# Cross-attention on one core: each norm's sum of squares folded over two partition halves, so that one constant matmul serves it

## What is computed

```python
text_p = x @ W_text + b_text;  audio_p = ctx @ W_audio + b_audio
Q = layer_norm(text_p, g1, beta1);  K = layer_norm(audio_p, g2, beta2);  V = audio_p
alpha = softmax(Q @ K.T / sqrt(512))
H = (alpha @ V) @ W_out + b_out
out = layer_norm(H + x, g_out, beta_out)
# layer_norm: (x - mean) * rsqrt(mean((x - mean)**2) + 1e-5) * gamma + beta
```

## Time and profile before

| | |
|---|---|
| time, median of 3 runs | 1315.46 us (1315.35 to 1315.54) |
| the profiled execution | 1315.32 us, its span 1313.5 us |
| PE busy | 1293.2 us (98%) |
| ACT busy | 1014.2 us (77%) |
| DVE busy | 934.8 us (71%) |
| POOL busy | 728.7 us (55%) |

### The profile page before, as it was taken

How to read it: one execution, slowest core, us unless ns; L and a number is a source line. 1 busy time by engine, 2 the same in 40 slices (tenths; PEclk the granted TensorE clock), 3 DMA queues, 4 the chain that set the end, 5 groups by cost and what they waited for, 6 DMA issues and landing times.

```text
span 1313.5 us, 22669 instructions
## 1 busy us (share of the span) xinstructions
PE 1293.2 (98%) x6960; PEld 1104.6 (84%) x6960; DVE 934.8 (71%) x1537; ACT 1014.2 (77%) x1655; POOL 728.7 (55%) x757
## 2 busy tenths in 40 slices
PE   7999999999999999999999999999999999999996
PEld 5688888888888888888888888888888888888885
DVE  6577666777667777667776667776667776667777
ACT  6678777788777887787887777887777887778873
POOL 1124666555675556675556665556665556755566
PEclk9999999999999999999999999999999999999999
DMA  7454755565755666745657655657655667555682
GB/s 248 121 123 126 200 179 135 155 186 184 200 174 119 170 180 196 199 139 148 169 176 200 192 145 138 188 176 200 185 122 164 184 184 200 166 134 163 180 205 81
DMA packets 76694, 221.04 MB, mean 168 GB/s; under 512 B 9856, under 2 KB 9856, under 8 KB 68480
## 3 DMA queue, kind: packets, MB, share of 16 engines
q1 hardware_dynamic: 55312, 154.70, 33.4%
q0 software_dynamic: 21360, 66.06, 26.4%
HBM read 121.12 MB, written 33.55 MB: 118 GB/s over the span
## 4 chain that ended last, share of the span: by engine, by line
PE 95%; DVE 2%; POOL 1%; DMA 1%; SPq 1%; ACT 1%; issue 0%; DVEq 0%; ACTq 0%
PE wide L295 9%; PE wide L294 9%; PE wide L293 9%; PE score L262 7%; PE score L260 7%; PE score L261 7%; PE wide L262 7%; PE wide L260 7%; PE wide L261 7%; PE wide L342 6%; PE wide L343 6%; PE wide L344 6%; PE score L267 2%; PE turn L262 1%; PE turn L261 1%; PE turn L260 1%
## 5 line engine op out<-in xcount | busy, mean ns | idle before, releaser
L954 POOL TENSOR_TENSOR y_rows<-y_rows,go_row 128x512 f32<-128x512 f32 x120 | 156.9, 1308 | 271.5 <-ACT y_rows L513 271.5
L293 PE MATMUL wide<-xT_hi,wt_hi 128*128 128x512 f32 x512 | 206.8, 404 | 0.7 <-ACT k_cols L482 0.7
L295 PE MATMUL wide<-xT_hi,wt_lo 128*128 128x512 f32 x512 | 202.0, 395 | 0.0
L294 PE MATMUL wide<-xT_lo,wt_hi 128*128 128x512 f32 x512 | 201.8, 394 | 0.0
L481 ACT ACTIVATE squares<-wide,bac_col 128x512 f32<-128x512 f32 x128 | 88.3, 690 | 116.9 <-PE wide L262 116.9
L956 POOL TENSOR_TENSOR y_rows<-y_rows,betao_row 128x512 f32<-128x512 f32 x120 | 165.6, 1380 | 9.4
L694 DVE SCALAR_TENSOR_TENSOR k_cols<-k_cols,g_col,turn 128x512 f32<-128x512 f32 x128 | 92.2, 742 | 100.7 <-ACT turn L499 100.7
L260 PE MATMUL wide<-cT_hi,wa_hi 128*128 128x512 f32 x384 | 152.4, 397 | 0.0
L342 PE MATMUL wide<-wao_hi,pcT_hi 128*128 128x512 f32 x384 | 151.8, 395 | 0.6 <-DVE pcT_lo L648 0.6
L262 PE MATMUL wide<-cT_hi,wa_lo 128*128 128x512 f32 x384 | 152.3, 397 | 0.0
L261 PE MATMUL wide<-cT_lo,wa_hi 128*128 128x512 f32 x384 | 152.1, 396 | 0.0
(11 more groups left out here) (121 smaller groups left out, 3575.2 us busy)
## 6 DMA issues: line engine op xcount, KB each, us to landing
xT_in<-in_xT SPq DMA_DIRECT2D x32, 1024.0 KB, 9.8
y_rows<-in_x_rows SPq DMA_DIRECT2D x124, 256.0 KB, 4.4
xT_lo<-xT_in POOLq DMA_DIRECT2D x31, 1024.0 KB, 7.0
y_rows<-bao_row POOLq DMA_DIRECT2D x31, 1024.0 KB, 10.9
out<-y_rows SPq DMA_DIRECT2D x124, 256.0 KB, 2.3
cT_in<-in_cT SPq DMA_DIRECT2D x32, 768.0 KB, 8.0
c_kept<-in_c_rows SPq DMA_DIRECT2D x32, 768.0 KB, 7.0
q_cols<-in_L_xattn_W_text SPq DMA_DIRECT2D x1, 1024.0 KB, 5.6
```

What stands on the lines that cost most here:

```text
L293: nc.tensor.matmul(wide[h][:], wt_hi[:, d, cols], xT_hi[:, d, :], start=(d == 0), stop=False)
L294: nc.tensor.matmul(wide[h][:], wt_hi[:, d, cols], xT_lo[:, d, :], start=False, stop=False)
L295: done = nc.tensor.matmul(wide[h][:], wt_lo[:, d, cols], xT_hi[:, d, :], start=False, stop=(d == DT - 1))
L954: nc.gpsimd.tensor_tensor(rows, rows, go_row[:], ALU.mult).then_inc(y_scaled, 1)
```

## The change

The 128x512 sum is folded to 64x512 before it is split. ACT copies its upper 64 partitions into the bank that the mean will later be written to (`move_half`), DVE adds them to the lower 64 (`sq_half`), and the split puts the high part in partitions 0 to 63 and the low part in partitions 64 to 127 of one tile `sq_parts`. One matmul with `mean_of` then sums both. The keys' mean matmul stands behind the whole of the query projection h=1 instead of behind its first quarter. Two waits of ACT are for the folded sum instead of the split one.

```diff
             def mean_squares(i, to, parts_made, var):
-                pe.wait_ge(sq_hi_made, i + 1)
-                nc.tensor.matmul(to, mean_of[:], sq_hi[:], start=True, stop=False)
-                pe.wait_ge(sq_lo_made, i + 1)
-                nc.tensor.matmul(to, mean_of[:], sq_lo[:], start=False, stop=True).then_inc(var, 1)
+                pe.wait_ge(parts_made, i + 1)
+                nc.tensor.matmul(to, mean_of[:], sq_parts[:], start=True, stop=True).then_inc(var, 1)
...
-                project_q(i, 1, 0)
-                mean_squares(i, turn[0][:], k_sq_hi, k_sq_lo, k_var)
-                project_q(i, 1, 2)
+                project_q(i, 1)
+                mean_squares(i, turn[0][:], k_sq_parts, k_var)
...
-                wait(act, q_sq_lo if h == 3 else q_summed, i)
+                wait(act, q_halved if h == 3 else q_summed, i)
...
-                act.wait_ge(k_sq_lo if h == 3 else k_summed, i + 1)
+                act.wait_ge(k_halved if h == 3 else k_summed, i + 1)
...
+            def move_half(i, to, summed, moved):
+                act.wait_ge(summed, i + 1)
+                nc.scalar.copy(to[P // 2:P, :], squares[P // 2:P, 3, :]).then_inc(moved, 1)
...
                 k_centre(i, 3)
+                move_half(i, turn[0], k_summed, k_moved)
                 if late:
                     y_norm(i - 2, odd, 0)
...
                 q_centre(i, 3)
+                move_half(i, turn[1], q_summed, q_moved)
                 k_high(i, 3)
...
-            def split_sum(i, var_before, before, summed, hi_made, lo_made):
+            def split_sum(i, of, moved, var_before, before, halved, hi_made, parts_made):
+                half = P // 2
+                dve.wait_ge(moved, i + 1)
+                nc.vector.tensor_tensor(sq_half[:], squares[0:half, 3, :], of[half:P, :], ALU.add).then_inc(halved, 1)
                 wait(dve, var_before, before)
-                dve.wait_ge(summed, i + 1)
-                nc.vector.tensor_copy(sq_hi[:], squares[:, 3, :]).then_inc(hi_made, 1)
+                dve.wait_ge(halved, i + 1)
+                nc.vector.tensor_copy(sq_parts[0:half, :], sq_half[:]).then_inc(hi_made, 1)
                 dve.wait_ge(hi_made, i + 1)
-                low(sq_lo[:], squares[:, 3, :], sq_hi[:]).then_inc(lo_made, 1)
+                low(sq_parts[half:P, :], sq_half[:], sq_parts[0:half, :]).then_inc(parts_made, 1)
```

More of the change, by code:

```diff
@@ L70, in cross_attention_kernel @@
         squares = sb("squares", [P, HT, T * P])
-        sq_hi, sq_lo = sb("sq_hi", [P, T * P], F32R), sb("sq_lo", [P, T * P], F32R)
+        sq_parts, sq_half = sb("sq_parts", [P, T * P], F32R), sb("sq_half", [P // 2, T * P])
         kT_hi, kT_lo = sb("kT_hi", [P, HT, T * P], F32R), sb("kT_lo", [P, HT, T * P], F32R)
@@ L122, in cross_attention_kernel @@
         mean_of_made = sem("mean_of_made")
+        k_moved, q_moved = sem("k_moved"), sem("q_moved")
         k_log, q_log, k_rstd, q_rstd = sem("k_log"), sem("q_log"), sem("k_rstd"), sem("q_rstd")
@@ L130, in cross_attention_kernel @@
         xT_split, cT_split, pT_split, pc_split = sem("xT_split"), sem("cT_split"), sem("pT_split"), sem("pc_split")
-        k_added, k_summed, k_sq_hi, k_sq_lo = sem("k_added"), sem("k_summed"), sem("k_sq_hi"), sem("k_sq_lo")
-        q_added, q_summed, q_sq_hi, q_sq_lo = sem("q_added"), sem("q_summed"), sem("q_sq_hi"), sem("q_sq_lo")
+        k_added, k_summed, k_halved = sem("k_added"), sem("k_summed"), sem("k_halved")
+        q_added, q_summed, q_halved = sem("q_added"), sem("q_summed"), sem("q_halved")
+        k_sq_hi, k_sq_parts, q_sq_hi, q_sq_parts = sem("k_sq_hi"), sem("k_sq_parts"), sem("q_sq_hi"), sem("q_sq_parts")
         k_normed, q_normed = sem("k_normed"), sem("q_normed")
@@ L297, in project_q, with mean_squares @@
                     done.then_inc(q_done, 1)
-            def mean_squares(i, to, sq_hi_made, sq_lo_made, var):
-                pe.wait_ge(sq_hi_made, i + 1)
-                nc.tensor.matmul(to, mean_of[:], sq_hi[:], start=True, stop=False)
-                pe.wait_ge(sq_lo_made, i + 1)
-                nc.tensor.matmul(to, mean_of[:], sq_lo[:], start=False, stop=True).then_inc(var, 1)
+            def mean_squares(i, to, parts_made, var):
+                pe.wait_ge(parts_made, i + 1)
+                nc.tensor.matmul(to, mean_of[:], sq_parts[:], start=True, stop=True).then_inc(var, 1)
             def turn_p(j, b):
@@ L403, in step @@
                     probs_context(j, 2)
-                mean_squares(i, turn[1][:], q_sq_hi, q_sq_lo, q_var)
+                mean_squares(i, turn[1][:], q_sq_parts, q_var)
                 if not first:
@@ L817, in step @@
                 sum_squares(i, k_squared, k_added, k_summed)
-                split_sum(i, q_var, i, k_summed, k_sq_hi, k_sq_lo)
+                split_sum(i, turn[0], k_moved, q_var, i, k_halved, k_sq_hi, k_sq_parts)
                 k_norm(i, 0)
@@ L830, in step @@
                 sum_squares(i, q_squared, q_added, q_summed)
-                split_sum(i, k_var, i + 1, q_summed, q_sq_hi, q_sq_lo)
+                split_sum(i, turn[1], q_moved, k_var, i + 1, q_halved, q_sq_hi, q_sq_parts)
                 if not first:
```

## The result

The changed kernel takes 1328.74 us (median of 4 runs, 1328.55 to 1328.79) against 1315.4 us of the kernel before on the same chip: ratio 1.0101, 95% interval 1.0084 to 1.0119. The forecast was 1324.2 us.

What follows compares the result with a forecast made beforehand. PE was taken as the bound, never waiting. Stalls 0.76 less gain 0.46 give +0.30 us a step: +9.2, less 0.5 in step 0, is +8.7 on 1315.32; with 0.14 for the median, 1324.2 us, range 1313 to 1331.

Steps and rivals of the forecast that it cites:

- PE is the bound, a matmul is worth 0.232 us: On PE, which never waits: two 512-column matmuls fewer a step save 0.464 us, 14.8 us over 32 steps.
- Full price for half the partitions: On ACT and DVE: 64-partition operations cost as much as 128-partition ones; copy 0.59, addition 0.69, cast 0.43, low part 0.69 us.
- The rival by which cost goes by partitions: Copy, addition, cast and low part at half price, 1.22 instead of 2.40 us; no stalls, 1300.7 us; chance 0.1 with other shorter chains.
- The keys' side has room: At the keys' mean matmul: low part ends at 664.0, PE comes at 665.22; slack 1.2 us, so no stall.
- POOL's lateness: POOL passes the queries' norm's 0.6 us delay to the next step's keys' sum; slack shrinks from 1.2 to 0.6, no stall.
- The queries' chain: From queries' sum to output product: copy and addition outlast the slack of some 1.1 us; PE stalls 0.76 us a step.
- `pc_low` starts behind the end: On DVE: `pc_low` starts 0.03 us after the low part's end, without overlap, 0.11 us later; 3.4 us in all.
- second rival: Stall and gain cancel, every disputed term at its lower end: -0.02 us a step, 1314.5 us; chance 0.13.
- the overlap of `pc_low`: On DVE: `pc_low` starts before the low part ends, as in the rows before, taking 0.11 us off the step.
- the free second matmul: On PE: the matmul after one that had to wait costs nothing extra, taking back 0.11 us a step.
- The mean matmul's wait and the output product's are one wait: On PE, queries' side: 0.16 us stall at the mean matmul counts within the 0.65 us total up to the output product.
- Steps 1 to 31 have this pattern: Each of these steps loses 0.30 us, stalls 0.76 less gain 0.46, making +9.2 us; step 0 gains 0.5 us.

Runs made afterwards that it cites:

- keys alone: Changed kernel with only the keys' sum folded, queries split whole with two matmuls as before; against the kernel before, 1308.38 us, ratio 0.9948.
- without the copy: Changed kernel whose queries' side has no ACT copy, DVE adding another SBUF half tile instead; against the kernel before, 1309.49 us, ratio 0.9957.
- same partitions: Changed kernel with the queries' copy, addition and low part kept in partitions 0 to 63; against the kernel before, 1324.19 us, ratio 1.0067.
- queries alone: Changed kernel with only the queries' sum folded, the keys' two matmuls in their old place; against the kernel before, 1331.51 us, ratio 1.0125.

## Why the prediction was right, point by point

- **PE is the bound, a matmul is worth 0.232 us.** Held: keys alone saves 7.0 us (32 x 0.232 = 7.4).
- **Full price for half the partitions.** Held: copy 0.586 (taken 0.59), addition 0.690 (0.69), cast 0.42 (0.43), low 0.685 on the queries' side (0.69), over 64 partitions each. The rival by which cost goes by partitions falls with these rows. The Trainium skill's rule (constant plus free elements; "VectorE: DVE Perf Modes", section on the TRN2 errata) agrees with them for VectorE.
- **The keys' side has room.** Held: no wait in the changed kernel, none with the keys folded alone. Its slack with POOL's lateness in it is 0.4, not 0.6: in the step shown above the keys' low part runs from 669.31 to 670.00, and PE comes at 670.43. In the two runs with a later queries' norm (the mean behind six matmuls) it is gone.
- **The queries' chain.** Held to 0.03 us at every point of the table above, in the step shown; the output product of every second step is 0.1 later. The sum was forecast as stalls of 0.76 and measured, in the mean of the steps, as 0.17 + 0.54 + 0.09 = 0.80; per step +0.30 forecast, +0.37 measured, of which 0.03 is the spread-out rest.
- **`pc_low` starts behind the end.** Held, and shown to hang on the partitions. It was worth more than the 3.4 us that I gave: 4.5 us in time, 0.14 in the step.
- **A slip in the second rival.** The terms that it takes back add up to 0.28, and 0.30 less 0.28 is +0.02 a step, about 1315.5 us, not -0.02 and 1314.5. It changes no other number. Of its terms the overlap of `pc_low` did not come, nor did the free second matmul (0.09), and the sum of squares was 0.08 late.
- **The mean matmul's wait and the output product's are one wait.** Held, by the run that moves the mean alone.
- **The total was 4.5 us short**, and this is the term of the sum that was mis-sized: "Steps 1 to 31 have this pattern: +9.2. In step 0 ... -0.5." The steps gave 30 x 0.367 = 11.0 instead of 30 x 0.295 = 8.9; and for what lies around them I had nothing but these -0.5. The last step and the end gave +2.6 (1.23 and 1.33).

The last step is different in a way that could have been read before. It leaves out nine matmuls of the output product, which come behind the scores, so PE is at the scores 2.1 us sooner, and the norm's lateness, hidden in all other steps, is bare there. PE's timeline of the changed kernel:

```profile
1292.28 0.38 PE L262 MATMUL score<-kT_hi,qT_hi 128*128 128x256 f32 x1 [0.70 <-DVE qT_lo L709]
...
1293.16 0.39 PE L262 MATMUL score<-kT_hi,qT_hi 128*128 128x256 f32 x1 [0.26 <-DVE qT_lo L709]
```

The stage from the scores to the next turn takes 7.46 us there instead of 6.63. The last `qT_lo` starts 1.88 us after the first score, before 1.04. Of these 0.84 us, 0.59 are there at the norm's first multiplication already. The other 0.25 come behind it and were not in my forecast: one `qT_lo` in every steady step, and in the last, now runs beside a POOL addition and takes 1.63 us, where before two of them took 0.99 and 1.13. DVE's and POOL's timelines, a steady step of the changed kernel:

```profile
684.69 1.40 DVE L703 SCALAR_TENSOR_TENSOR q_cols<-q_cols,g_col,turn 128x512 f32<-128x512 f32 x2
686.23 1.62 DVE L709 SCALAR_TENSOR_TENSOR qT_lo<-q_cols,beta_col,qT_hi 128x512 fp32r<-128x512 f32 x1
...
684.32 1.61 POOL L963 TENSOR_TENSOR y_rows<-y_rows,go_row 128x512 f32<-128x512 f32 x1 [8.40 <-ACT y_rows L517]
686.01 1.30 POOL L965 TENSOR_TENSOR y_rows<-y_rows,betao_row 128x512 f32<-128x512 f32 x1
```

The 1.33 us behind PE's last matmul: POOL's and DVE's timelines of the changed kernel,

```profile
1314.02 1.30 POOL L980 TENSOR_TENSOR xT_in<-xT_in,go_row 128x512 f32<-128x512 f32 x1 [0.93 <-ACT xT_in L632]
...
1314.11 1.76 DVE L774 SCALAR_TENSOR_TENSOR y_rows<-y_rows,y_sc,betao_row 128x512 f32<-128x512 f32 x1 [0.28 <-issue]
```

DVE's operation takes 1.76 us instead of 0.75, beside one of POOL that started just ahead of it. In the kernel before, DVE was first by 0.26 and took 0.75, and POOL's took 1.63. In all twelve traces the two go together: POOL is first in eight (the changed kernel, without the copy, same partitions and the five with the mean matmul later) and the end takes 12.0 to 12.1 us from PE's last matmul; DVE is first in four (the kernel before, keys alone, queries alone, the keys' mean moved alone) and it takes 10.7 to 10.8. No run was made for it; that the two engines' order decides it is argued from this, not shown by an edit.

## What to carry to other kernels

Taking an instruction from the engine that sets the time is worth its place in the stream only if the wait that follows keeps its slack: here PE came 0.23 us sooner and its data 1.5 us later, at a place with 1.1 us of slack. Price an edit at each wait behind it on the engine that got longer; what was lost was not the sum itself but `pc_low`, which merely stood behind it in DVE's order. And when it is lost that way, look for what can change places: work that was ready went into the idle time, the waiting matmul was moved by single matmuls, and the same fold turned from 1.0% slower to 0.9% faster.

## What the runs showed of the hardware that was not expected

- Two DVE operations in a row overlap by about 0.08 us, and lose that where the second starts in other partitions than those before it, in what it reads from PSUM or in what it writes: 0.61 against 0.72 from start to start.
- Of a DVE and a POOL operation over 128x512 tiles that run side by side, the one that starts second is stretched where DVE's operation reads two tensors, both in SBUF. In the changed kernel `qT_lo` takes 1.63 us instead of 0.74 behind a POOL addition of 1.29 us (30 times), and POOL takes 1.62 instead of 1.3 behind DVE's `kT_lo` of 0.74 (30 times). `q_cols`, which reads one tensor from SBUF and one from PSUM, keeps its 0.74 beside POOL (60 times).
